# Cross attention and a 4-bit feed-forward layer on one core: a second PSUM bank for wide query jobs, and the mask and the exponents of the scores in PSUM

## What is computed

```python
q = apply_rope(heads(layernorm(x) @ wq, 32))            # (b, 32, 256, 128)
k = apply_rope(heads(ctx @ wk, 8)); v = heads(ctx @ wv, 8)
scores = einsum('bhqd,bhkd->bhqk', q, repeat(k, 4)) / sqrt(128)
attn = softmax(scores + mask[:, None], axis=-1)
x = x + merge(einsum('bhqk,bhkd->bhqd', attn, repeat(v, 4))) @ wo
e = norm(layernorm(x)); w_l = dequant(qweight, lut4, 4); w_h = dequant(qweight, lut8, 8)
x = x + where(e > 64, layernorm(x) @ w_h.T, layernorm(x) @ w_l.T) + bias
```

## Time and profile before

| | us |
|---|---|
| median of 3 runs | 2418.38 |
| lowest, highest | 2414.87, 2420.93 |
| the profiled execution | 2415.12 |
| its span in the profile | 2413.3 |
| TensorE busy | 2363.8 |
| VectorE, ScalarE, POOL busy | 1647.8, 1152.2, 544.7 |
| mean granted TensorE clock | 1.0 |

### The profile page before, as it was taken

One profiled execution on the slowest core, in us unless ns is written; L12 is line 12 of the kernel. 1 busy time (PEld: TensorE's weight loads), 2 busy tenths in 40 slices (PEclk: granted clock), 3 DMA queues, 4 the chain that ended last, 5 costly groups with the idle time before them and its releaser, 6 DMA issues.

```text
span 2413.3 us, 35106 instructions
## 1 busy us (share of the span) xinstructions
PE 2363.8 (98%) x11990; PEld 2000.5 (83%) x11990; DVE 1647.8 (68%) x3808; ACT 1152.2 (48%) x2475; POOL 544.7 (23%) x674
## 2 busy tenths in 40 slices
PE   9999999999999999999999999999999999999999
PEld 8998998787878787878888888888888888887887
DVE  8887776666666666766666667666667666665553
ACT  5555544546455555555544544444454445444110
POOL 1000001232222222222222222222222222222111
PEclk9999999999999999999999999999999999999999
DMA  7466567544434343434447633343333334335211
GB/s 260 155 211 200 179 213 251 162 120 116 114 106 130 97 135 97 125 105 124 117 147 235 204 100 105 97 119 91 105 105 101 105 90 116 101 86 181 88 70 53
DMA packets 322033, 320.91 MB, mean 133 GB/s; under 512 B 31552, under 2 KB 258112, under 8 KB 321856
## 3 DMA queue, kind: packets, MB, share of 16 engines
q1 hardware_dynamic: 321856, 318.68, 44.0%
HBM read 181.73 MB, written 71.30 MB: 105 GB/s over the span
## 4 chain that ended last, share of the span: by engine, by line
PE 66%; DVE 12%; POOL 6%; ACT 6%; DMA 4%; issue 3%; SPq 2%; DVEq 0%; ACTq 0%
PE bank L789 18%; PE bank L867 16%; PE bank L751 7%; PE bank L905 7%; PE bank L728 7%; POOL probs L1822 5%; PE bank L839 5%; PE bank L805 4%; ACT probs L1182 3%; DVE residual L1703 3%; DVE probs L1661 2%; SPq L591 2%; DMA small_split<-probs 2%; DVE probs L1677 2%; DMA raw<-in_L_xattn_wq 1%
## 5 line engine op out<-in xcount | busy, mean ns | idle before, releaser
L789 PE MATMUL bank<-acts_split,weights_split 128*128 128x512 f32 (+1 forms) x3168 | 751.5, 386 | 30.6 <-DVE rope_a L1622 30.2
L867 PE MATMUL bank<-weights_split,small_split 128*128 128x512 f32 x3072 | 741.1, 390 | 4.9 <-DVE small_split L1687 4.9
L789 PEld LDWEIGHTS bank<-acts_split,weights_split 128*128 128x128 f32 x3168 | 566.4, 188 | 144.3 <-DVE rope_a L1622 22.6
L867 PEld LDWEIGHTS bank<-weights_split,small_split 128*128 128x128 f32 x3072 | 574.2, 188 | 125.3 <-DVE small_split L1687 6.2
L1822 POOL TENSOR_SCALAR probs<-probs,row_numbers 128x256 f32<-128x256 f32 x512 | 336.2, 668 | 1301.9 <-DVE row_numbers L1673 1301.9
L1182 ACT ACTIVATE probs<-probs,row_numbers 128x256 f32<-128x256 f32 x512 | 256.5, 502 | 339.9 <-DVE row_numbers L1668 339.8
L1661 DVE CUSTOM_DVE_ANT_0 probs<-bank,mask_tile 128x256 f32<-128x256 f32 x512 | 197.2, 423 | 125.5 <-PE bank L805 124.4
L1677 DVE STREAM_TRANSPOSE probs<-probs 128x512 f32<-128x512 f32 x250 | 176.9, 708 | 127.0 <-POOL probs L1822 127.0
L1814 POOL TENSOR_TENSOR rope_x<-rope_x,sin_t 128x512 f32<-128x512 f32 (+1 forms) x132 | 165.9, 1256 | 377.3 <-ACT rope_x L1164 376.4
L1682 DVE TENSOR_TENSOR small_split<-small_split 128x512 fp32r<-128x512 f32 x250 | 186.8, 747 | 91.2 <-ACT small_split L1195 91.2
L805 PEld LDWEIGHTS bank<-small_split 128*128 128x128 f32 x1536 | 218.5, 190 | 24.4 <-DVE small_split L1633 1.8
(11 more groups left out here) (120 smaller groups left out, 2318.3 us busy)
## 6 DMA issues: line engine op xcount, KB each, us to landing
small_split<-probs SPq DMA_DIRECT2D x1000, 64.0 KB, 2.2
raw<-in_L_xattn_wq SPq DMA_DIRECT2D x61, 512.0 KB, 3.5
raw<-in_L_xattn_wo SPq DMA_DIRECT2D x60, 512.0 KB, 3.9
k_scratch<-small_split SPq DMA_DIRECT2D x64, 256.0 KB, 2.3
v_scratch<-small_split SPq DMA_DIRECT2D x32, 512.0 KB, 2.9
x_scratch<-raw SPq DMA_DIRECT2D x64, 256.0 KB, 2.8
acts_split<-x_scratch SPq DMA_DIRECT2D x32, 512.0 KB, 5.1
mask_tile<-in_mask_BxSxS_ff SPq DMA_DIRECT2D x64, 256.0 KB, 3.0
```

Source lines behind the costliest of these rows:

```text
L789: last = pe.matmul(query_bank(j)[:, 0:wide], wq_s[:, h, c, a, :], xT[:, c, m, b * S:b * S + wide], start=c == 0 and i == 0, stop=c == C - ...
L867: last = pe.matmul(out_ps[part][:, :], o_s[:, a, u % 2 * S + t * P:u % 2 * S + (t + 1) * P], wo_s[:, h, m, n * BANK:(n + 1) * BANK], start ...
```

## The change

It has six parts.

1. `query_bank`: wide jobs use banks 2 and 3 in turn. Job j waits for the cosine product of job j - 2.
2. The bank that no query job uses at the moment (`spare_bank`) takes the turned halves of a row tile, and the squares, one after the other in the same 512 columns. Query jobs that would overwrite them get waits. The six units that TensorE turns use bank 2 (unit 1: bank 3).
3. The square root of a row tile goes to the middle of step 8 on ScalarE, with a one-element exponential behind it that brings the table of the exponential back. `row_var` comes right after the mask of step 8, `row_scale` at the end of step 8.
4. The load of weight piece 8 no longer waits for the squares and is issued before `move_blocks` of step 7.
5. `add_mask` reads the scores packed and writes the sum back into bank 0. The exponents read it there, with a stride of four words, and write `probs`. The scores of u wait for the exponents of u - 1. The wait for the moved blocks of u - 2 is the exponents'. The host stores the mask as it is.
6. The columns of `probs` are grouped so that both row halves of a block stand together (64 columns). Attention reads 8 runs of 64 in place of 16 runs of 32. One split of an output weight goes from step 2 to step 3 in the first round.

```diff
-    LOAD_LAST = (6, 8)
+    LOAD_LAST = (6,)
...
-        pT_keys = R[:, 4608:6656].rearrange("p (l q k j) -> p l k q j", l=2, k=TS, j=QUAD)
+        pT_keys = R[:, 4608:6656].rearrange("p (l a k n) -> p l k a n", l=2, k=TS, n=TS * QUAD)
...
-        prob_parts = prob_t[:, :].rearrange("p (s b t m) -> p s t b m", s=2, b=P // QUAD, t=TS)
+        prob_parts = prob_t[:, :].rearrange("p (s b k t i) -> p s t b k i", s=2, b=P // QUAD, k=TS, t=TS)
...
         def query_bank(j):
-            return q_ps[j % 2 if j < REP else 0]
+            if j < REP:
+                return q_ps[j % 2]
+            return (bank[2], bank[3])[j % 2]
+        def turn_bank(u):
+            return bank[3] if u == 1 else bank[2]
+        def spare_bank(u):
+            j, = (n for at in (u, u - 1) for n, chunks in WORK[at] if chunks[0] == 0)
+            return query_bank(j + 1 if u % 2 else j - 1)
...
                 if u + 1 in PIECE and (u + 1) % UNITS in LOAD_LAST:
-                    if u + 1 in ROW_AT:
-                        sp.wait_ge(row_step, 4 * ROW_AT[u + 1] + 4)
                     load_weights(u + 1)
...
-                    pe.wait_ge(rope_cosd, 2 + A_ROPES + (j - 1 if j <= REP else j))
+                    pe.wait_ge(rope_cosd, 2 + A_ROPES + j - 1)
+                    for squares in (u - 1 for u in ROW_AT if u <= units[0]):
+                        if WORK[squares + 1][0][0] == j:
+                            pe.wait_ge(row_step, 4 * ROW_AT[squares + 1] + 4)
+                    for rows in (u for u, side in SIDE.items() if u < units[0] and side[1] == 0):
+                        if WORK[rows + 1][0][0] == j:
+                            pe.wait_ge(x_lo, 2 * SIDE[rows][0] + 1)
+                        if WORK[rows + 3][0][0] == j:
+                            pe.wait_ge(x_lo, 2 * SIDE[rows][0] + 2)
...
             def scores(u):
-                pe.wait_ge(s_read, u + 1)
+                pe.wait_ge(exp_done, u)
...
-            def turn_side(e, j):
+            def turn_side(u):
+                e, j = SIDE[u]
+                job = WORK[u][0][0]
+                pe.wait_ge(rope_cosd, 2 + A_ROPES + job)
...
-                    last = pe.transpose(pT_ps[:, c * P:(c + 1) * P],
+                    last = pe.transpose(spare_bank(u)[:, c * P:(c + 1) * P],
...
                 for n, total in enumerate((x_var0, x_var1)):
-                    act.activation(spare[n], ln_row[:, n * BANK:(n + 1) * BANK], ACT.Square, scale=float(D) ** -0.5,
+                    if n and len(spare) == 1:
+                        act.wait_ge(row_step, 4 * e + 3)
+                    act.activation(spare[n % len(spare)], ln_row[:, n * BANK:(n + 1) * BANK], ACT.Square, scale=float(D) ** -0.5,
                                    accum_out=total).then_inc(row_step, 1)
...
             def exponent(u):
+                if u == 0:
+                    act.wait_ge(d_stored, 16)
+                if u - 2 in PE_TURNS:
+                    act.wait_ge(pT_tr, PE_TURNS.index(u - 2) + 1)
+                elif u >= 2:
+                    act.wait_ge(pT_in[u % 2], 4 * 16 * landed(u - 2))
                 act.wait_ge(s_max, u + 1)
                 for t in range(TS):
-                    row = prob_part(u, t)
-                    last = act.activation(row, row, ACT.Exp,
+                    row, scored = probs[:, u % 2, t, :], s_ps[:, t * S:(t + 1) * S]
+                    if u not in PE_TURNS:
+                        row = prob_parts[:, u % 2, t]
+                        scored = scored.rearrange("p (k i b) -> p b k i", k=TS, i=QUAD)
+                    last = act.activation(row, scored, ACT.Exp,
...
+                if u in ROW_AT:
+                    row_root(ROW_AT[u])
+                    act.wait_ge(row_step, 4 * ROW_AT[u] + 4)
+                    act.activation(x_mean, x_mean, ACT.Exp, scale=0.0)
                 if u in SIDE:
                     act.wait_ge(w_lo, A_PIECES + PIECE_AT[max(at for at in PIECE if at < u)] + 1)
-                    x_high(*SIDE[u], pT_ps)
+                    x_high(*SIDE[u], spare_bank(u))
...
                 if u + 1 in ROW_AT:
-                    act.wait_ge(w_lo, A_PIECES + PIECE_AT[max(at for at in PIECE if at <= u)] + 1)
-                    act.wait_ge(x_stored, 4 * 16 * ROW_AT[u + 1])
-                    row_square(ROW_AT[u + 1], [raw_t[:, n * BANK:(n + 1) * BANK] for n in range(2)])
-                if u in ROW_AT:
-                    row_root(ROW_AT[u])
+                    act.wait_ge(rope_cosd, 2 + A_ROPES + WORK[u][0][0])
+                    row_square(ROW_AT[u + 1], [spare_bank(u)[:, :]])
...
             def add_mask(u):
-                if u - 2 in PE_TURNS:
-                    dve.wait_ge(pT_tr, PE_TURNS.index(u - 2) + 1)
-                elif u >= 2:
-                    dve.wait_ge(pT_in[u % 2], 4 * 16 * landed(u - 2))
-                if u == 0:
-                    dve.wait_ge(d_stored, 16)
                 dve.wait_ge(s_mm, 1 + u + 1)
                 for t in range(TS):
                     last = dve.tensor_tensor_reduce(
-                        out=by_blocks(probs[:, u % 2, t, :]) if u in PE_TURNS else prob_part(u, t),
-                        in0=by_blocks(s_ps[:, t * S:(t + 1) * S]),
-                        in1=mask_t[:, t, :].rearrange("p (b m) -> p b m", b=P // QUAD), scale=1.0, ...
+                        out=s_ps[:, t * S:(t + 1) * S], in0=s_ps[:, t * S:(t + 1) * S],
+                        in1=mask_t[:, t, :], scale=1.0, ...
...
                 if u < NU - 1:
                     add_mask(u)
+                if u in ROW_AT:
+                    row_var(ROW_AT[u])
...
+                if u == 3:
+                    output_weights_lo(3)
...
-                if u == 2:
-                    output_weights_lo(3)
...
                 if u in ROW_AT:
-                    row_var(ROW_AT[u])
-                if u - 1 in ROW_AT:
-                    row_scale(ROW_AT[u - 1])
+                    row_scale(ROW_AT[u])
...
-    arrays["mask_BxSxS2_ff0"] = np.ascontiguousarray(
-        arrays["mask_BxSxS2_ff0"].reshape(nb, s, s // 4, 4).transpose(0, 1, 3, 2)).reshape(nb, s, s)
```

More of the change, by code:

```diff
@@ L253, in build_xattn_ffn @@
         s_ps = bank[0]
-        pT_ps = bank[2]
-        pT_cols = bank[2][:, :].rearrange("p (a t k j) -> p t k a j", t=TS, k=TS, j=QUAD)
         o_ps = bank[5]
@@ L825, in turn @@
                     pe.wait_ge(x_lo, 2 * NT)
+                    pe.wait_ge(rope_cosd, 2 + A_ROPES + (DONE[u] + 1 if u in DONE else len(JOBS)))
+                else:
+                    pe.wait_ge(rope_cosd, 2 + A_ROPES + AHEAD + 1)
                 for t in range(TS):
                     for k in range(TS):
-                        last = pe.transpose(pT_cols[:, t, k], probs[:, u % 2, t, k * P:(k + 1) * P], ident[:, :])
+                        last = pe.transpose(pT_cols(u)[:, t, k], probs[:, u % 2, t, k * P:(k + 1) * P], ident[:, :])
                 last.then_inc(pT_tr, 1)
@@ L849, in attend_one @@
                     for i, (a, m) in enumerate(PASSES):
-                        last = pe.matmul(o_ps[:, half_of], v_s[:, k, a, :], pT_keys[:, m, k, u % 2 * (S // QUAD):(u % 2 + 1) * (S // QUAD)],
+                        last = pe.matmul(o_ps[:, half_of], v_s[:, k, a, :], pT_keys[:, m, k, u % 2 * (P // QUAD):(u % 2 + 1) * (P // QUAD)],
                                          start=k == 0 and i == 0, stop=k == TS - 1 and i == 2)
@@ L1190, in turned_high @@
                     act.wait_ge(pT_tr, PE_TURNS.index(u) + 1)
-                    source = pT_ps[:, :]
+                    source = turn_bank(u)[:, :]
                 else:
@@ L1644, in split_piece @@
                 weights_split(A_PIECES + PIECE_AT[at], kind, h)
-            def by_blocks(row):
-                return row.rearrange("p (m b) -> p b m", b=P // QUAD)
             def add_mask(u):
@@ L1679, in turned_low @@
             def turned_low(u):
[L1680 removed]
+                source = turn_bank(u)[:, :] if u in PE_TURNS else pT_s[:, LO, u % 2, :].bitcast(F32)
                 dve.wait_ge(pT_hi, u + 1)
@@ L1741, in _ @@
                 if u in SIDE:
-                    x_low(*SIDE[u], pT_ps)
+                    x_low(*SIDE[u], spare_bank(u))
                 if u in DONE and u not in LATE:
```

12 lines of the change are left out of this document (8 added, 4 removed).

## The result

The changed kernel takes 2387.87 us (median of 4 runs, 2386.78 to 2388.45), the kernel before beside it on the same chip 2416.62 us (2411.98 to 2420.93). The ratio is 0.9881, with a 95% interval of 0.9861 to 0.9901: faster by 28.8 us, where the forecast had 25.4 less than the median (2393, range 2376 to 2411). All medians are of fast executions: one of the six of banks_alone took 6554.47 us and is left out.

A forecast was written before the change was run, and what follows sets the result against it. TensorE, busy 2363.8 of 2413.3 us, bounds the kernel. Terms 2.8 + 0.9 + 13.3 + 3.6 + 3.8 = 24.4 us off the profiled 2415.1 give 2390.7; against the median 2394, rounded down to 2393, range 2376 to 2411.

The forecast's parts named there:

- What bounds the kernel: TensorE, busy 2363.8 of 2413.3 us; its stops before the query matmuls cost 38 us, 2.0 of them in step 4.
- Part 1, step 8, rounds 7 to 14: Second query bank: 0.45 us slack, less 0.3 for load competition, plus 0.2 for cheaper exponents: 0.35 x 8 = 2.8 us.
- Part 1, step 8, rounds 1 to 6: Second query bank: the query waits for the squares instead and starts 0.15 us earlier a round, 0.9 us in all.
- The other steps: Second query bank, remaining even steps: 16.3 us of stops, less 2.0 for attention's waits and 1.0 for late blocks: 13.3 us.
- Ends: First and last round: half of 7.2 us of stops before the query kept, 3.6 us, because projections wait for VectorE too.
- Part 2: Norm-row steps moved into step 8: the move costs nothing; its worth is that 12.2 us in steps 10, 12 stay won.
- Part 3: Mask and exponents in PSUM: mask write 0 (bounds -30, +215 ns), exponent -36 ns; scores waiting for exponents free.
- Part 4: Attention reading runs of 64: half of 12 ns, less where TensorE waits right behind: 5 ns x 762 = 3.8 us.
- (a): Rival: time handed back, stops reappear before attention in every even step; 2410 to 2416 us, chance 0.11.
- (b): Rival: free load, full ends, free runs of 64, no late blocks: 14 us more off, 2379 us; chance 0.18.
- (c): Rival: slow strided exponent, +215 ns each, stops TensorE 0.36 us in 128 even steps, 46 us: 2439 us; chance 0.09.
- What was to show it: Signs if right: query waits nearly gone, squares' stop 0.8 us, turned_low waits 8 to 12, attention 396 ns, mask 420, exponent 465.

The follow-up runs named there:

- banks_alone: Kernel before plus the second query bank, squares and side rows in the free bank, load not waiting for squares; the rest as before: 2401.85 us, ratio 0.9950.
- u_load: Changed kernel with the load of weight piece 8 back behind the block moves of step 7, not waiting for the squares: 2387.32 us, ratio 0.9886.
- u_wait: Changed kernel with wide query jobs waiting again for the cosine product of the job just before, banks still alternating: 2402.21 us, ratio 0.9950.
- u_psum: Changed kernel with the mask's sum written to probs and the exponents taken in place there again: 2384.04 us, ratio 0.9880.
- p_packed: Changed kernel with exponents reading PSUM packed instead of with a stride of four words, columns and keys not matching: 2387.78 us (one run).
- u_norm: Changed kernel with square root, variance and scale steps of a row tile put back to their old places: 2398.25 us, ratio 0.9942.
- n_both: Changed kernel with squares written to a small SBUF tile, and mask and exponents in SBUF as before: 2382.06 us, ratio 0.9869.
- n_waste: Changed kernel with squares written to a small SBUF tile, the next query not waiting for them: 2384.83 us, ratio 0.9879.

## Why the prediction was right

**What bounds the kernel: right.** TensorE's stops were what there was to gain. The 38 us before the query were there: by the starts of every step of rounds 0 to 14 (the time from scores to query, less 0.71) they are 38.6, of which 1.9 in the steps 4 of rounds 1 to 14, as forecast.

**Part 1, step 8, rounds 7 to 14: right in size, with two errors that cancel by luck.** Forecast 0.35 us a round, 2.8 in all; measured 8.79 - 8.41 = 0.38, 3.0 in all. The row shows the mechanism:

```profile
1360.96 0.69 DVE L1714 TENSOR_TENSOR small_split<-small_split 128x512 fp32r<-128x512 f32 x1 [0.60 <-ACT small_split L1235]
...
1361.70 1.66 PE L867 MATMUL bank<-small_split 128*128 128x512 f32 x6 [0.50 <-DVE small_split L1714]
```

This is the stop that I worked out as 0.60 us from the earlier trace rows; by the starts it is 0.60 to 0.66 in six of the eight rounds, near 1.0 in the others. But the 0.3 us charged for the load that competes were nothing (u_load), and the 0.2 us credited for cheaper exponents did not come, since the mask took back what they gave.

**Part 1, step 8, rounds 1 to 6: wrong by half.** Forecast 0.9 us, measured 6 x 0.07 = 0.4, no more than the table can tell. The term took the squares' end from the trace of before. They end 0.30 us later; the wait between them was priced right (0.1), but not that the chain in front of them would be 0.14 us later.

**The other steps: more than forecast.** Forecast 13.3 us. Measured in rounds 1 to 6 (2.56 - 0.07) x 6 = 14.9 and in rounds 7 to 14 (1.05 - 0.38) x 8 = 5.4, 20.3 in all; less some 4 us that runs of 64 add here it is 16. The most came from steps 10 and 12 of rounds 1 to 6 (0.89 and 1.16 us) and from steps 4 and 12 of rounds 7 to 14 (0.44 us each). In that step 4 the query stood for 0.14 us alone; the other 0.3 are two stops before attention, in rounds 9 and 13, that went as well, and shorter attention. Part of what came off in steps 10 and 12 of rounds 1 to 6 came off without the second bank (u_wait). Step 6 goes the other way, 7.61 to 7.98 us (7.72 in the second trace). It is held in three of those eight rounds (one more in rounds 1 to 6), by blocks that land late, the case for which the prediction took off 1.0 us; in rounds 7 to 14 it is 0.37 x 8 = 3.0. The worst is round 12:

```profile
1785.50 0.88 PE L826 MATMUL bank<-small_split 128*128 128x256 f32 x6
...
1786.57 0.63 ACT L1235 ACTIVATE small_split<-small_split 128x512 fp32r<-128x512 f32 x1 [2.34 <-DMA small_split<-probs]
```

In other rounds this high half begins before the scores of step 6 (in round 9, 0.97 us before). Why the blocks are late there, and in no step 6 of the kernel before, is open.

**Ends: right.** Forecast 3.6; measured 4.1 + 0.2 = 4.3. One wait that the prediction declared free isn't free here: scores behind exponents. In steady state it is, but in the first round the exponents of unit 2 wait for the first blocks. What the stop costs in the end isn't shown: the first round takes 113.4 us in u_psum without this wait, and 113.9 to 116.0 in four traces with it (the change twice, u_load, p_packed).

```profile
415.45 0.20 ACT L1222 ACTIVATION_READ_ACCUMULATOR probs<-bank,row_numbers 128x1 f32 x1
...
415.79 0.95 PE L826 MATMUL bank<-small_split 128*128 128x256 f32 x6 [2.54 <-ACT probs L1222]
```

**Part 2: right in size, its account incomplete.** It was costed at nothing, with the remark that 12.2 us would be handed back in steps 10 and 12 without it. u_norm hands back 12.9, mostly there. But the prediction took these 12.2 us for the second bank's, which the moved steps only keep. u_wait shows steps 10 and 12 shorter by 0.87 and 0.75 us without the freed wait, so part of them was not the bank's to give. The new waits around the side rows cost nothing that shows: step 14 of rounds 1 to 6 goes from 8.10 to 8.06 us.

**Part 3: probably wrong in sign, small in size.** Forecast: a credit of 0.2 us in step 8, all else free. The strided read is free, as taken. The write was taken at 0 with bounds of -30 and +215 ns: the mask costs 23 more, and its accumulator read 56 more, which no term had. What it adds up to lies between 1.3 (u_psum) and 2.8 us (n_both against n_waste) lost. The two together make the loss likely, neither shows it alone, and at which steps it arises isn't settled: single traces scatter as much.

**Part 4: the price right by luck, its working wrong.** Half of the 12 ns was taken, 3.8 us; runs of 64 cost nothing, 8.0 us by the starts, and 4.6 to 5.6 arrive. The allowance "less where TensorE waits right behind" was the larger effect.

**The rivals.** (a), handed back: out, attention's listed stops rose from 5.5 to 12.7 us, not by 25. The u_norm run shows that the danger was real in rounds 1 to 6, and that part 2 is what prevents it. (b), more comes off (2379): its two items of the load and of the runs hold as mechanisms, the ends did not gain in full. The result of 2387.9 lies between it and the forecast. (c), the strided exponent: out, 470 against 471 ns.

**What was to show it.** Met: the query's waits for the cosine product gone (30.2 to 1.0 us), no table load before the exponent of step 9, attention at 397 ns (396 forecast). Near: the exponent at 470 (465), the squares' stop at 1.05 to 1.21 us by the starts (0.8), attention's waits for turned_low at 6.6 us (8 to 12). Missed: the mask at 445 (420), and scores that wait for an exponent, which the prediction had among the signs of (c) and which here is one stop of 2.5 us in the first round.

## What to carry to other kernels

Count a stop from the starts of the instructions, step by step and round by round (the mean of a stage hides stops of single rounds), and ask which wait ends next: a second buffer gave 12.4 us alone, and moving small steps of other engines out of the way of that next wait was worth 12.9 more, part of which may have come without the buffer. Undoing one part of a finished change prices it in the new kernel, where the old wait stops a step 4 for 0.47 us and not for 0.14; what a part gives by itself takes a run of its own. A gain on the bounding engine is paid out only in steps where it doesn't already wait: here 5 of 8 us. Before an intermediate goes to another memory, price its write and the accumulator read, not only the read that gets cheaper.

## What the runs showed of the hardware

A mask with maximum (VectorE, 256 columns, PSUM and SBUF in) takes 422 to 423 ns when it writes SBUF and 445 when it writes PSUM, and the accumulator read behind it 84 and 140 ns. A matmul of 512 moving columns starts the next after 237 ns when it reads runs of 32 columns, and after 227 with runs of 64, as packed. ScalarE reads PSUM with a stride of four words in the time of a packed read (470 and 471 ns). A POOL instruction of 0.48 us that reads SBUF takes 0.91 to 1.02 beside a VectorE subtraction with both inputs in SBUF that began first; where POOL's began 0.1 to 0.2 us ahead, the subtraction takes 0.9 us instead of 0.69.
